# Attention passes of a graph kernel: eight groups in the buffer of selections by node, 48 row places instead of 56, and another place for requests and register loads on ScalarE

## What is computed

```python
q = h @ Wq + bq;  k = h @ Wk + bk;  v = h @ Wv + bv       # 4 heads of 32
k_j = k[src] + e                                          # e = edge_weight @ We
alpha = einsum('ehc,ehc->eh', q[tgt], k_j) / sqrt(32)
amax = segment_max(alpha, tgt)
ex = exp(alpha - amax[tgt])
denom = segment_sum(ex, tgt)
out = segment_sum((v[src] + e) * (ex / denom[tgt]), tgt)
x_r = h @ Wskip + bskip
beta = sigmoid(concat([out, x_r, out - x_r]) @ Wbeta)
h = relu(batchnorm(beta * x_r + (1 - beta) * out)) + h    # two rounds
```

## Time and profile before

| | us |
|---|---|
| median of 3 runs | 8874.65 (8861.37 to 8881.97) |
| the profiled execution, its time | 8870.64 |
| its span, first to last instruction | 8868.6 |
| first attention pass, first gather to last | 4279.5 to about 6360 |
| second attention pass, first gather to last | about 6590 to 8655.7 |

### The profile page before, as it was taken

The page is one execution under the profiler, slowest core; times in us unless marked ns, Lnnn a source line. Parts: engine busy times, 40 slices in busy tenths (PEclk is TensorE's granted clock), DMA queues, the critical chain, the costliest instruction groups (busy, mean ns, idle before and its releaser), DMA issues. The chain is left out here.

```text
span 8868.6 us, 130681 instructions
## 1 busy us (share of the span) xinstructions
PE 5228.6 (59%) x25255; PEld 4456.5 (50%) x25255; DVE 3724.6 (42%) x10780; ACT 3202.4 (36%) x13039; POOL 6271.6 (71%) x6563
## 2 busy tenths in 40 slices
PE   2555555557555555554666666666666666666666
PEld 2444444445444444443555555555455555555553
DVE  4000000002000000003677777777787777777778
ACT  4555555553333333333322222222222222222222
POOL 4777777773777777776677777777657777777776
PEclk8676676667555555556777777777787777777777
DMA  5555555556434444445666767667546666766673
GB/s 177 176 178 174 171 178 176 177 176 227 121 121 123 124 124 121 122 129 157 196 212 212 217 207 218 210 213 217 180 141 212 215 214 211 218 208 216 210 218 107
DMA packets 748040, 1597.27 MB, mean 180 GB/s; under 512 B 194927, under 2 KB 402184, under 8 KB 727292
## 3 DMA queue, kind: packets, MB, share of 16 engines
q10 hardware_dynamic: 344768, 846.48, 28.6%
q0 software_dynamic: 249536, 614.81, 24.5%
q1 hardware_dynamic: 152956, 127.62, 4.7%
HBM read 1268.68 MB, written 319.67 MB: 179 GB/s over the span
## 5 line engine op out<-in xcount | busy, mean ns | idle before, releaser
L1742 POOL DMA_INDIRECT conv_held<-key_value,conv_src x3128 | 2996.9, 958 | 1235.3 <-issue 934.6
L2092 ACT ACTIVATE conv_kv<-conv_held 128x256 f32 x3320 | 1093.7, 403 | 2575.8 <-PE conv_ps_sums L1979 1371.4
L891 POOL DMA_INDIRECT second_msg<-sage_hidden_projected,second_src x1516 | 1430.3, 943 | 586.5 <-issue 458.7
L891 POOL DMA_INDIRECT first_msg<-sage_in,first_src x1564 | 1475.8, 944 | 498.9 <-issue 475.5
L1979 PE MATMUL conv_ps_sums<-conv_kv,conv_sel 128*128 128x136 f32 x6640 | 1379.2, 365 | 565.5 <-DVE sums L1889 521.7
L1979 PEld LDWEIGHTS conv_ps_sums<-conv_kv,conv_sel 128*128 128x128 f32 x6640 | 1195.5, 258 | 723.5 <-DVE sums L1889 530.6
L1964 PE MATMUL conv_ps_query<-query_table,conv_selT 128*128 x6640 | 1228.3, 342 | 557.8 <-DMA conv_selT<-selections_turned 444.2
L1964 PEld LDWEIGHTS conv_ps_query<-query_table,conv_selT 128*128 128x128 f32 x6640 | 1080.4, 243 | 636.1 <-issue 634.0
L1109 PE MATMUL second_ps_sums<-second_msg,second_sel 128*128 x3328 | 832.4, 430 | 794.4 <-ACTq L961 793.3
L1109 PE MATMUL first_ps_sums<-first_msg,first_sel 128*128 x3328 | 712.3, 379 | 865.9 <-ACTq L961 865.1
L1889 DVE TENSOR_TENSOR sums<-sums,conv_ps_sums 128x136 f32 x3320 | 970.8, 292 | 572.8 <-DVE sums L1889 221.0
(11 more groups left out here) (270 smaller groups left out, 4520.8 us busy)
## 6 DMA issues: line engine op xcount, KB each, us to landing
conv_selT<-selections_turned ACTq DMA_DIRECT2D x414, 512.0 KB
conv_sel<-selections ACTq DMA_DIRECT2D x414, 512.0 KB
selections<-first_sel ACTq DMA_DIRECT2D x52, 2048.0 KB
selections_turned<-first_selT ACTq DMA_DIRECT2D x416, 256.0 KB
second_sel<-selections ACTq DMA_DIRECT2D x104, 1024.0 KB, 5.2
conv_held<-key_value,conv_src POOLq DMA_INDIRECT x3128
first_msg<-sage_in,first_src POOLq DMA_INDIRECT x1564
second_msg<-sage_hidden_projected,second_src POOLq DMA_INDIRECT x1516
```

Source lines behind the costliest of these rows:

```text
L891: pool.indirect_dma_start(msg[:, to * MW:to * MW + D], None, table, bass.IndirectOffsetOnAxis(ap=src[:, lap % 2, j:j + 1], axis=0)).then_i ...
L1742: pool.indirect_dma_start(held[:, (g * GR + i) % HELD, :], None, t.kv_d, bass.IndirectOffsetOnAxis(ap=src[:, lap % 2, j:j + 1], axis=0)).t ...
L2092: last = act.activation(kv[:, place_of_step(c * CH + j), :], held[:, bass.ds(from_tiles[j % (CH // 2)], 1), :].rearrange("p a d -> p (a d) ...
```

## The change

The ring for `sel` gets a size of its own, eight groups instead of four, and `PLACES` goes from 56 to 48, which takes the same room back. `select` then waits only for the sums of the chunk before `b`. On ScalarE, its four requests move from the head of `stages`, from behind copy 3 and from behind copy 5 to two pairs behind copy 1 and copy 2. The 16-register loads become a function `tiles_of`; that for copies 0 to 3 of a chunk moves to a place ahead of copy 7 of the chunk before, that for copies 4 to 7 to a place ahead of copy 3. Copy n waits for the sums of group n - 12.

```diff
-PLACES = 56
+PLACES = 48
...
+SELS = KG
...
-        sel = sb("sel", [P, SELG, GR, P])
+        sel = sb("sel", [P, SELS, GR, P])
...
-                                pe.wait_ge(sel_in[k // 2 % (SELG // 2)], 16 * ((KG * c + k) // SELG) + 16)
+                                pe.wait_ge(sel_in[k // 2], 16 * c + 16)
...
-                            last = pe.matmul(sums_of(h, step), sel[:, k % SELG, step % GR, :],
+                            last = pe.matmul(sums_of(h, step), sel[:, k, step % GR, :],
...
-                    half = q % (SELG // 2)
-                    act.wait_ge(sums_ready, KP * c + 2 * (2 * q + 1) + 2 + 2 * KP - 2 * SELG)
+                    act.wait_ge(sums_ready, KP * (c - 1) + 2 * (2 * q + 1) + 2 + 2 * KP)
...
+                def tiles_of(a, half):
+
+                    c, h, g = a
+                    if half == 0:
+                        act.wait_ge(list_in[h], 16 * g + 16)
+                    regs = [act.alloc_register(f"{tag}_held{c}_{half}_{i}") for i in range(CH // 2)]
+                    act.load(regs, lists[0:1, h, half * (CH // 2):(half + 1) * (CH // 2)])
+                    from_tiles[half] = [act.snap(r, donate=True, min_val=0, max_val=HELD - 1) for r in regs]
...
                 def stages(a, b, following):
...
-                    select(b, 0)
-                    select(b, 1)
                     if a is not None:
                         select_turned(a, 1)
                         copy(a, 0)
...
                         copy(a, 1)
+                    select(b, 0)
+                    select(b, 1)
+                    if a is not None:
                         copy(a, 2)
+                    select(b, 2)
+                    select(b, 3)
+                    if a is not None:
+                        tiles_of(a, 1)
                         copy(a, 3)
                     if after is not None:
                         weights(after)
                     if a is not None:
                         select_turned(a, 3)
-                    select(b, 2)
-                    if a is not None:
                         copy(a, 4)
                         copy(a, 5)
-                    select(b, 3)
...
                         copy(a, 6)
                     if following is not None:
                         select_turned(following, 0)
+                    if following is not None:
+                        tiles_of(following, 0)
                     if a is not None and groups(a) == KG:
                         copy(a, 7)
```

More of the change, by code:

```diff
@@ L1675, in conv_edges @@
             [sem(f"{k}{h}") for h in range(2)] for k in ("wd_in", "blk_in", "src_in", "list_in"))
-        sel_in, selT_in = ([sem(f"{k}{q}") for q in range(SELG // 2)] for k in ("sel_in", "selT_in"))
+        sel_in, selT_in = ([sem(f"{k}{q}") for q in range(n // 2)] for k, n in (("sel_in", SELS), ("selT_in", SELG)))
         gathered = [sem(f"gathered{k}") for k in range(HELD_GROUPS)]
@@ L2042, in select @@
                     lo, hi = 2 * q, min(2 * q + 2, groups(b))
-                    half = q % (SELG // 2)
-                    act.wait_ge(sums_ready, KP * c + 2 * (2 * q + 1) + 2 + 2 * KP - 2 * SELG)
-                    act.dma_start(sel[:, 2 * half:2 * half + hi - lo, :, :].rearrange("p k i w -> p (k i w)"),
+                    act.wait_ge(sums_ready, KP * (c - 1) + 2 * (2 * q + 1) + 2 + 2 * KP)
+                    act.dma_start(sel[:, lo:hi, :, :].rearrange("p k i w -> p (k i w)"),
                                   t.sel_d[bass.ds(c, 1), :, lo * GR * P:hi * GR * P]
-                                  .rearrange("a p w -> p (a w)")).then_inc(sel_in[half], 16)
+                                  .rearrange("a p w -> p (a w)")).then_inc(sel_in[q], 16)
                 def select_turned(a, q):
@@ L2072, in records @@
                     act.dma_start(stp[:, h, :, :], t.step_d[c * CH:c * CH + CH, :].partition_broadcast(P)).then_inc(wd_in[h], 16)
-                from_tiles = []
+                from_tiles = {}
+                def tiles_of(a, half):
[5 more added lines that the diff above has]
+                    from_tiles[half] = [act.snap(r, donate=True, min_val=0, max_val=HELD - 1) for r in regs]
                 def copy(a, k):
@@ L2079, in copy @@
                     n = KG * c + k
[L2080 to L2085, removed]
                     tiles = act.value_load(lists[0:1, h, CH + k:CH + k + 1], min_val=1, max_val=GROUPS)
@@ L2092, in copy @@
                         last = act.activation(kv[:, place_of_step(c * CH + j), :],
-                                              held[:, bass.ds(from_tiles[j % (CH // 2)], 1), :].rearrange("p a d -> p (a d)"), ACT.Copy)
+                                              held[:, bass.ds(from_tiles[j // (CH // 2)][j % (CH // 2)], 1), :].rearrange("p a d -> p (a d)"), ACT.Copy)
                     last.then_inc(copied, 1)
@@ L2138, in _ @@
                 select_turned(first, 1)
+                tiles_of(first, 0)
+                tiles_of(first, 1)
                 copy(first, 0)
@@ L2151, in _ @@
                 copy(first, 6)
+                tiles_of(chunk(0, 1), 0)
                 copy(first, 7)
```

## The result

The changed kernel takes 8934.8 us (median of 4 runs, 8927.3 to 8944.1), the kernel before 8869.8 us in the same session (8861.4 to 8882.0): **1.0072, interval 1.0056 to 1.0088**, 65 us slower. The profiled execution of the changed kernel has a span of 8931.7 us against 8868.6, so it carries 63 of the 65 us.

The account below looks back on a forecast made before the run. GpSimd's gathers were taken to bound the attention passes. Landings +61 and +20, lone requests -13, copies -13 and -20 gave +35 us on 8870.6, 8906; with 4 us for the median 8909 us, range 8805 to 8980.

Parts of the forecast that it names:

- rival A: The forecast itself, the burst of requests moves and grows, with its smaller and larger forms: +20 to +90 us; chance 0.45.
- The bound: In the two attention passes GpSimd is the fullest engine; its 200 us of stalls are all a better order could win.
- Allowed landing 4.8 us: At GpSimd's gathers, a group's landing may take at most 4.8 us before the next dependent gather has to wait.
- Part 1: Requests for sel move behind the exponential: landing stalls +61 us, +20 left at the old place, -13 from lone requests.
- The proportion 3 / 2: Part 1's estimate: landing stalls of 123 us grow as the crowded stretch does, 3 MB against 2, +61 us.
- the doubling: Part 1's upper bound: each MB beyond the first counts alike, so twice the present landing stall, +123 us.
- the old crowd: Four 512 KB requests close together around the exponential, 110 of 123 us of landing stalls; 0.2 us per chunk left, +20.
- the signs: What would show it right, among them GpSimd's stalls lying 3 to 14 us after the exponential, hardly any at the old place.
- Parts 3 and 4, copies: ScalarE's copies 4 and 5 come earlier, -13 us; copy 6's stalls partly covered because GpSimd is late more often, -20 us.
- Part 2, copy 2: ScalarE's copy 2 comes 0.6 us later behind two more issues; taken at 0, without cover 40 us.
- the bound of 14: Sign for ScalarE's order: copy 4 starts less than 14 us after the exponential.
- Rival B: Faster: gathers get their DMA turns whatever the queue holds, and the old crowd is gone; -65 us, 8810; chance 0.26.

Follow-up runs that it names:

- The fastest kernel: Changed kernel with requests for sel spread further (none beside another), 20 tiles in held and 44 row places: 8707.7 us, 0.9798 of the kernel before.

## Why the prediction was right, and where its sum was off

The forecast was 8909 us, by a burst that "moves and grows"; the measured 8935 us is that case (rival A), 65 us over the kernel before, in the upper half of its +20 to +90.

- **The bound**, GpSimd with its stalls as all that can be won: right. In all thirteen kernels the gathers' busy and idle time together follow the span; what is left of the span stays between 4633 and 4656 us. The fastest kernel won 182 us of the span in its profiled execution (179 in the medians), where the bound was 200.
- **Allowed landing 4.8 us**: right. In the groups that a landing stalled, the time from last gather to landing less the stall is 4.83 us in the median before and 4.84 after, and hardly a group seen within 4.5 us stalled GpSimd. With one group more, 7.4 us cost nothing. What the account leaves out is that the landing counts only through SyncE's order, see above.
- **Part 1**: landings +61 + 20 - 13 = +68 forecast, +84 measured. The requests stand where it put them, `sel` at 1.4, 1.8, 3.3 and 3.7 us after the exponential, but turned 3 comes at 11.3 us (forecast 7 to 9), since copy 3 ahead of it is late. The proportion 3 / 2 was too small, the doubling too large. Groups whose last gather falls in the crowd took 5.8 us on the mean before (28 to 32 us after the exponential) and take 6.9 and 6.5 us now, for 8 us of each chunk: both the lateness and the time for which it lasts grew, and the forecast's reason named only the second. That 3 / 2 came within 16 us is in part luck: the rows allowed anything from nothing to +123, and the prediction said so. Of the old crowd 21 us are left, as taken; all of the new stalls lie 5 to 14 us after the exponential, as the signs asked.
- **Parts 3 and 4, copies**: -33 forecast, -31 measured. The run with an eighth of the bytes shows why: they are hidden, not cured.
- **Part 2, copy 2**: 0.7 us later (median start 3.0 us after the exponential, before 2.3), forecast 0.6; VectorE's waits for copies rise from 430.0 to 492.9 us and cost nothing that the span shows, since the gathers' line accounts for all of it. Copy 3 was forecast 2.5 us later and is 3.7 us (10.5 against 6.8), because its tiles land late. Copy 4 starts at 13.7 us in the median (16.5): the bound of 14 holds, barely; the gain of 5 to 7 us is 3, for the same reason.
- **The term that was missing**: gathers that are longer themselves, +16.9 us. The sum took 0.95 us for each. With it and the 14 us by which the idle time was undersized (net +49 against +35), 35 becomes 66, against 63 in the span.
- **Rival B**, turns whatever the queue holds (the Trainium skill, DMA: Bandwidth & Descriptors, section on queues, rings and completion order, from which that rule came): landings of 6.9 us on the mean in the first 4 us behind the exponential, and of 3.9 us there with an eighth of the bytes in the same requests, speak against it as an estimate of time. Its other half was right: the 86 us of copies that GpSimd did not feel; 44 us of copy stalls came back in that run, forecast 43.

Open is what within the DMA engines makes a gather wait; the runs tell bytes from requests and packets, not more.

## What to carry to other kernels

A wait that seems to be only a limit of a buffer may be what keeps large requests apart: before a larger buffer takes it away, say where the requests will then stand, and place them one by one. Where an engine stands for late landings, look first at how many it may have under way, and at what frees a place: one more group in the ring made the burst harmless and was worth more than any order of the requests. Here the places were held by a loop that released one group only behind the landing of another; to turn that round is the cheaper thing to try, and it is untried. When a stall is taken away, count what it had hidden, here half of SyncE's waits for copies.

## What was not expected of the hardware

A gather's instruction on GpSimd can get longer beside a run of VectorE's multiplications. VectorE's timeline beside the gather of 2.20 us that starts at 7935.43:

```profile
7932.51 4.29 DVE L1792 TENSOR_TENSOR conv_kv<-conv_kv 128x512 f32<-128x512 f32 x7
7936.73 0.68 DVE L1764 TENSOR_TENSOR conv_kv<-conv_ps_query,conv_kv 128x512 f32<-128x512 f32 x1
...
7937.61 0.68 DVE L1769 TENSOR_REDUCE conv_score<-conv_kv 128x16 f32<-128x512 f32 x1
```

It ends at 7937.63, where the reduction begins. Of 3128 gathers 121 take over 1.1 us (before: 114), every one of them beside L1792 and 30 of them on into L1764; what they take over 0.945 us is 51 us (before: 33). The kernel before has no such gather that reaches into the multiplication. Not every gather beside L1792 is longer: it is 121 of 329, and 112 of 486 before, where all of the 112 start in the first half of the run and none of the 221 that start in its second half is longer. The stalled gathers of the burst start later, at the end of the run of L1792, where the multiplication for group 3 follows at once, and the longest takes 3.20 us (before: 1.48). With the burst and 20 tiles no gather reaches into the multiplication, with an eighth of the bytes 2 do, with two requests behind the exponential 37: so these gathers come with the stall behind the burst. The Trainium skill (SBUF — State Buffer, section on SBUF's two separate sides) says that a VectorE instruction with two inputs in SBUF holds a port pair that it shares with GpSimd, against a GpSimd instruction that reads SBUF, and that one with at most one input in SBUF does not contend with GpSimd. L1792 has two inputs in SBUF, and the longer gathers stand beside it; but by that alone the second half of its run should lengthen them too, which it does not in the kernel before. L1764 reads one input from PSUM, and still 30 gathers last into it. So the trace agrees with the section in part only, and no run here took this apart.
